# A graph network on one core: destination rows are added onto source rows by an accumulating DMA instead of by VectorE

## The chip, the core and the metric

The kernel runs on 1 core of a Trainium2 chip (trn2). The metric is device time in microseconds of one execution, the median of several runs. The profile is one execution, taken by the hardware profiler; its times count from the span's start.

## What is computed

The reference takes 3125 nodes with 256 features, 53125 edges (sorted by destination) with 128 features each, and runs four graph blocks, each followed by a residual sum and a layer norm. The change lies in the first, the edge network:

```
h = concat(x[src], x[dst])                     # per edge, 512 wide
h = tanh(h @ W0 + b0)                          # 512 -> 406
h = tanh(h @ W1 + b1)                          # 406 -> 323
h = h @ W2 + b2                                # 323 -> 256
h = h * (edge_attr @ Wg)                       # 128 -> 256, a gate
out = mean of h over the edges of each source node
x = layernorm(x + out)
```

The other three blocks are a GCN pair, three SAGE layers, and a mean aggregation of a linear layer, all on the same edges.

## The kernel before, in words

**Tables.** Because `concat(x[src], x[dst]) @ W0` is a sum of two products, a setup stage (25 tiles of 128 nodes, loop over `n < T`) computes two tables in HBM, `p_tab = x @ W0[:256]` and `q_tab = x @ W0[256:] + b0`, with rows of `H1 = 416` float32 numbers. For each tile TensorE (PE) runs 12 matmuls (L272 to L274), ScalarE (ACT) copies one half out of PSUM (L329) and VectorE (DVE) adds `b0` to the other (L398). The setup also counts the edges per bucket. It ends near 107 us.

**Edge stage.** 53248 edges (padded) are worked in `G = 104` groups of `GC = 4` chunks of `C = 128` edges. The stage is a software pipeline: each engine has one `body(t)` for turn t, written out by hand in the engine's own order and run by `edge_loop` (a few turns unrolled, then a hardware loop of 2 turns per iteration, then a few turns). `t.group(k)` is the group that is k ahead of the turn's own. In turn t:

- GpSimd (POOL) issues 12 indirect DMAs of 128 rows each: four gathers of source rows (`p_tab` to `p_in`) and four of destination rows (`q_tab` to `q_in`) for group t+3 (`gather`, L617), and four scatters of finished messages for group t-2 (`scatter`, L624). Between the three bursts of four it waits: for `s_L2` and `s_add` ahead of the first, for `s_L1` (TensorE has finished the first third of the layer W1 of group t) ahead of the second, for `s_place`, `s_L2` and `s_msg` ahead of the third.
- VectorE adds the two rows of group t+2, chunk by chunk (`add`, two instructions: L834 for 384 columns, L837 for the last 32 columns, which it writes four times side by side, so that `pre1` has 512 columns). It also takes the low halves of the hidden layers for the split products (`first_low` L853 and L855, `second_low` L867), the one-hots and places (L878 to L898), and the message, product times gate (L906).
- TensorE transposes `pre1` of group t+1 (L673, four per chunk), runs W1 on group t (`first`, L679 to L681 and L695) and W2 and the gate product on group t-1 (`second`, L679 to L681 and L712), and the rank products (L716).
- ScalarE runs tanh of the first hidden layer (L772, L774), of the second (L786, L789) and copies the gate out of PSUM (L798).

All of `pre1` and the gate lie in `R_buf`; `p_in`, `q_in` and `pre1` have two slots each. Two PSUM banks serve the second product: TensorE's `second(t, 2)` waits until the message of chunk 0 has been read out (`s_msg`), which waits for ScalarE's gate copy, which waits for TensorE's `s_L2`.

**After it** (from 2170 us): one-hot matmuls that build the counts and sum the messages, and the three further blocks. The change doesn't touch them, beyond where `pre1` is stored.

## Time and profile before

| what | value |
| --- | --- |
| median of 3 runs | 3755.33 us (3738.34, 3755.33, 3803.82) |
| span of the profiled execution | 3707.1 us |
| lowest run less that span | 31.2 us |
| median less that span | 48.2 us |
| busy: PE, DVE, ACT, POOL | 3298.7, 2156.1, 1576.1, 1363.5 us |
| edge stage (first gather to last scatter) | 108.5 to 2162 us |

How to read it: the profile gives no device time of its own beside its span, so what lies around the span is known only as the difference to the runs. Busy times are sums over the whole span; the edge stage is a little over half of it, and almost all of POOL's work lies there. The three runs differ by 1.7%.

### The profile page before, as it was taken

Reading aid. Unit: us, or ns where it says so; the run is one execution under the profiler, and the core shown is the slowest. Engines: PE = TensorE matmul, PEld = TensorE weight load, DVE = VectorE, ACT = ScalarE, POOL = GpSimd, SP = SyncE. Lnnn points to the kernel's source line nnn. Section 1 sums busy time; section 2 is a strip of 40 time slices with the busy share of each in tenths; the row PEclk is TensorE's granted clock in tenths of the full one; section 3 lists DMA queues with packets and bytes.
Section 4 is the critical chain, followed back from the end, with each engine's and each line's share of the span. In section 5 each row is a group of like instructions: output and inputs, shape, how many; then the busy total and the mean of one; then the engine's idle time right before and its main releaser. Section 6 shows DMA issues by size and latency. Waiting matters only on the chain. (4 is left out here: it accounts for less than half of the span.)

```text
span 3707.1 us, 68629 instructions
## 1 busy us (share of the span) xinstructions
PE 3298.7 (89%) x19277; PEld 2783.2 (75%) x19278; DVE 2156.1 (58%) x5404; ACT 1576.1 (43%) x3210; POOL 1363.5 (37%) x1410
## 2 busy tenths in 40 slices
PE   7688888888888888888888889899999999999999
PEld 6466766777767666767676766777888999999888
DVE  7566666666666665666666668899444211124422
ACT  2344545554555444555454547777111111111244
POOL 2556666666666555666665422222000000000000
PEclk9799999999999999999999989999999999999999
DMA  4444444444444433444444368888755666666465
GB/s 159 138 124 129 129 129 130 136 132 126 134 133 134 124 119 118 129 132 132 135 125 120 97 190 254 253 263 264 228 176 176 205 210 211 205 218 203 144 206 163
DMA packets 288343, 605.46 MB, mean 163 GB/s; under 512 B 38577, under 2 KB 195850, under 8 KB 288266
## 3 DMA queue, kind: packets, MB, share of 16 engines
q1 hardware_dynamic: 170848, 321.14, 28.0%
q0 software_dynamic: 73216, 232.67, 20.7%
q10 hardware_dynamic: 44202, 50.63, 4.0%
q8 instruction: 47, 0.77, 0.1%
q14 instruction: 30, 0.25, 0.0%
HBM read 493.97 MB, written 110.32 MB: 163 GB/s over the span
## 5 line engine op out<-in xcount | busy, mean ns | idle before, releaser
L998 PE MATMUL bank<-ring,parts 128*128 128x320 f32 x4000 | 641.6, 316 | 5.4 <-issue 2.5
L998 PEld LDWEIGHTS bank<-ring,parts 128*128 128x128 f32 x4000 | 595.1, 188 | 16.3 <-issue 10.9
L679 PE MATMUL bank<-w2h,hidden2h 108*128 108x256 f32 x1248 | 421.0, 337 | 143.1 <-DVE rows_out L906 112.0
L624 POOL DMA_INDIRECT msgs<-rows_out,sidx x416 | 427.5, 1028 | 306.9 <-PE bank L712 157.4
L617 POOL DMA_INDIRECT p_in<-p_tab,gidx x416 | 402.1, 967 | 289.2 <-issue 125.6
L617 POOL DMA_INDIRECT q_in<-q_tab,gidx x416 | 408.7, 982 | 231.3 <-issue 116.1
L679 PE MATMUL bank<-hidden1h,w1h 128*108 128x512 f32 x936 | 422.1, 451 | 23.7 <-DVE hidden2l L867 22.0
L679 PEld LDWEIGHTS bank<-w2h,hidden2h 108*128 108x128 f32 x1248 | 248.6, 199 | 194.0 <-DVE rows_out L906 142.4
L680 PE MATMUL bank<-hidden1l,w1h 128*108 128x512 f32 x936 | 382.6, 409 | 0.1
L681 PE MATMUL bank<-hidden1h,w1l 128*108 128x512 f32 x936 | 380.0, 406 | 0.0
L681 PE MATMUL bank<-w2h,hidden2l 108*128 108x256 f32 x1248 | 366.1, 293 | 4.2 <-issue 4.1
L673 PE MATMUL bank<-ident,R_buf 128*128 128x128 f32 x1664 | 254.3, 288 | 128.5 <-DVE hidden1h L855 97.2
L786 ACT ACTIVATE hidden2h<-bank,b1c 108x512 fp32r<-108x512 f32 (+1 forms) x312 | 215.2, 690 | 359.2 <-remote 177.3
L680 PE MATMUL bank<-w2l,hidden2h 108*128 108x256 f32 x1248 | 365.4, 293 | 2.9 <-issue 2.9
L1135 PE MATMUL bank<-at_dst,at_src 128*128 128x320 f32 x1088 | 324.8, 380 | 36.9 <-DVE at_src L1107 29.8
L867 DVE TENSOR_TENSOR hidden2l<-bank,hidden2h 108x512 fp32r<-108x512 f32 (+1 forms) x312 | 215.6, 691 | 234.8 <-ACT bank L789 216.6
L673 PEld LDWEIGHTS bank<-ident,R_buf 128*128 128x128 f32 x1664 | 209.3, 149 | 177.5 <-issue 134.5
L772 ACT ACTIVATE hidden1h<-bank 128x512 fp32r<-128x512 f32 x416 | 247.4, 595 | 216.3 <-remote 139.4
L798 ACT COPY R_buf<-bank 128x256 f32<-128x256 f32 x416 | 148.2, 376 | 439.6 <-PE bank L712 292.7
L1139 PE MATMUL bank<-R_buf,at_src 128*128 128x257 f32 x1088 | 325.1, 380 | 0.0
L906 DVE TENSOR_TENSOR rows_out<-bank,R_buf 128x256 f32<-128x256 f32 x416 | 166.6, 421 | 258.6 <-ACT R_buf L798 179.4
L1101 DVE TENSOR_SCALAR at_dst<-T_buf,R_buf 128x640 fp32r<-128x640 f32 x544 | 303.9, 559 | 11.5 <-PE bank L1139 9.3
(243 smaller groups left out, 6137.6 us busy)
## 6 DMA issues: line engine op xcount, KB each, us to landing
ring<-counts SPq DMA_DIRECT2D x250, 800.0 KB, 4.3
R_buf<-msgs SPq DMA_DIRECT2D x544, 130.0 KB, 3.0
counts<-cells ACTq DMA_DIRECT2D x125, 320.0 KB, 3.4
eT<-in_edge_T SPq DMA_DIRECT2D x104, 256.0 KB
p_in<-p_tab,gidx POOLq DMA_INDIRECT x416
q_in<-q_tab,gidx POOLq DMA_INDIRECT x416
msgs<-rows_out,sidx POOLq DMA_INDIRECT x416
p_tab<-p_out SPq DMA_DIRECT2D x25, 208.0 KB, 1.9
```

Of the source, the lines that this page charges most:

```text
L617: pool.indirect_dma_start(out=rows_in[:, z, c], out_offset=None, in_=tab[:], in_offset=bass.IndirectOffsetOnAxis(ap=gidx[:, z, which, c:c ...
L624: pool.indirect_dma_start(out=msgs[:], in_=rows_out[:, z, c], in_offset=None, out_offset=bass.IndirectOffsetOnAxis(ap=sidx[:, z, c:c + 1], ...
L673: mm = pe.transpose(bT[c % 2][:, k * C:(k + 1) * C], pre1[:, z, c, k * P:(k + 1) * P], ident[:])
L679: pe.matmul(out, lh.bitcast(F32R), rh.bitcast(F32R), start=first, stop=False)
L680: pe.matmul(out, lh.bitcast(F32R), rl.bitcast(F32R), start=False, stop=False)
L681: return pe.matmul(out, ll.bitcast(F32R), rh.bitcast(F32R), start=False, stop=last)
L772: act.activation(hidden1h[:, z, :, e].bitcast(F32R), src, ACT.Tanh).then_inc(s_hi1, 1)
L867: v.tensor_tensor(hidden2l[0:rows_m, z, m].bitcast(F32R), bH[m % 2][0:rows_m, :], hidden2h[0:rows_m, z, m], ALU.subtract).then_inc(s_lo2, 1)
L998: mm = pe.matmul(banks[q][:, 0:NW], part[:, TB * i + a, h * P:(h + 1) * P].bitcast(dt), ring[:, slot, a].bitcast(dt), start=first and x == ...
L1101: v.tensor_scalar(at_dst[:, u % HOTS].bitcast(F32R), iota[:], rows[:, u % RS, D + 2:D + 3], None, ALU.is_equal)
L1135: pe.matmul(bank[:, half * 512:half * 512 + 2 * CW][:, bass.ds(at[u], NW)], at_src[:, u % HOTS].bitcast(F32R), at_dst[:, u % HOTS, half * ...
L1139: pe.matmul(bS[:, bass.ds(at[u], SW)], at_src[:, u % HOTS], rows[:, u % RS, 0:SW], start=False, stop=False, skip_group_check=True).then_in ...
```

## The change

VectorE's `add` goes. POOL first gathers the source rows straight into `pre1`, and one turn later gathers the destination rows onto them with an accumulating indirect DMA (`compute_op=ALU.add`), so that `pre1` is complete when the DMA has landed. `pre1` gets its own buffer with a ring of four slots (`RING`), with source rows fetched four groups ahead and destination rows three. `p_in` and `q_in` go. Since nothing writes the last 32 columns four times any more, the tables themselves have 512 columns (`H1W`): W0 and b0 are widened on the host by repeating those columns, and the setup's matmuls, copies and table writes are 512 wide. POOL waits for `s_p_rows` (source rows landed) and `s_T` (slot transposed) where it waited for `s_add`; TensorE waits for `s_q_rows`, one semaphore for two chunks, where it waited for `s_add`. The copy of the row numbers (`table_rows`) moves to after `first_low(t, 3)`. POOL, TensorE and VectorE run hardware loops of four turns instead of two. The message scatters share one semaphore per slot.

```diff
--- before.py
+++ after.py
@@
+H1W = H1T * P
...
+RING = 4
...
-        p_tab, q_tab = dram("p_tab", [NP, H1]), dram("q_tab", [NP, H1])
+        p_tab, q_tab = dram("p_tab", [NP, H1W]), dram("q_tab", [NP, H1W])
...
-                                to, q = psum[2 * (n % 3) + half][:, 0:H1], 2 * half + k
+                                to, q = psum[2 * (n % 3) + half][:, 0:H1W], 2 * half + k
...
-                        act.copy(p_out[:, j], psum[2 * (n % 3)][:, 0:H1]).then_inc(s_pe, 1)
+                        act.copy(p_out[:, j], psum[2 * (n % 3)][:, 0:H1W]).then_inc(s_pe, 1)
...
-                        v.tensor_tensor(q_out[:, n % TB], psum[2 * (n % 3) + 1][:, 0:H1], b0_b[:],
+                        v.tensor_tensor(q_out[:, n % TB], psum[2 * (n % 3) + 1][:, 0:H1W], b0_b[:],
...
-            p_in, q_in = (esb(n, [P, 2, GC, H1]) for n in ("p_in", "q_in"))
-            pre1 = R_buf[:, 0:2 * GC * H1T * P].rearrange("p (z c n) -> p z c n", z=2, c=GC)
-            gate = R_buf[:, 2 * GC * H1T * P:][:, 0:GC * D].rearrange("p (c n) -> p c n", c=GC)
-            gidx = esb("gidx", [P, 2, 2, GC], I32)
+            pre1 = esb("pre1", [P, RING, GC, H1W])
+            gate = R_buf[:, 0:GC * D].rearrange("p (c n) -> p c n", c=GC)
+            gidx = esb("gidx", [P, RING, 2, GC], I32)
...
-            s_in_rows = [[esem(f"s_in_rows{z}{c}") for c in range(GC)] for z in range(2)]
-            s_sc = [[esem(f"s_sc{z}{c}") for c in range(GC)] for z in range(2)]
+            s_p_rows = [esem(f"s_p_rows{z}") for z in range(2)]
+            s_q_rows = [[esem(f"s_q_rows{y}{h}") for h in range(GC // 2)] for y in range(RING)]
+            s_sc = [esem(f"s_sc{z}") for z in range(2)]
             s_eT = [esem(f"s_eT{z}") for z in range(2)]
-            s_idx, s_add, s_T, s_th1, s_lo1 = (esem(n) for n in ("s_idx", "s_add", "s_T", "s_th1", "s_lo1"))
+            s_idx, s_T, s_th1, s_lo1 = (esem(n) for n in ("s_idx", "s_T", "s_th1", "s_lo1"))
...
-                def gather(t, c, tab, which, rows_in):
-
-                    z = t.slot(3)
-                    pool.indirect_dma_start(out=rows_in[:, z, c], out_offset=None, in_=tab[:],
-                                            in_offset=bass.IndirectOffsetOnAxis(ap=gidx[:, z, which, c:c + 1], axis=0)
-                                            ).then_inc(s_in_rows[z][c], 16)
+                def gather_source(t, c):
+
+                    y = t.ring(4)
+                    pool.indirect_dma_start(out=pre1[:, y, c], out_offset=None, in_=p_tab[:],
+                                            in_offset=bass.IndirectOffsetOnAxis(ap=gidx[:, y, 0, c:c + 1], axis=0)
+                                            ).then_inc(s_p_rows[t.slot(4)], 16)
+
+                def add_destination(t, c):
+
+                    y = t.ring(3)
+                    pool.indirect_dma_start(out=pre1[:, y, c], out_offset=None, in_=q_tab[:],
+                                            in_offset=bass.IndirectOffsetOnAxis(ap=gidx[:, y, 1, c:c + 1], axis=0),
+                                            compute_op=ALU.add).then_inc(s_q_rows[y][c // 2], 16)
 
...
                 def body(t):
 
                     if t.has(-2) and t.has(1):
                         pool.wait_ge(s_L2, t.group(-2) * GC + 3)
-                    if t.has(3):
-                        pool.wait_ge(s_idx, t.group(3) + 1)
-                        wait(pool, s_add, (t.group(3) - 1) * GC)
+                    if t.has(4):
+                        pool.wait_ge(s_idx, t.group(4) + 1)
+                        wait(pool, s_T, (t.group(4) - RING + 1) * GC)
                         stand_alone(pool, s_up)
                         for c in range(GC):
-                            gather(t, c, p_tab, 0, p_in)
+                            gather_source(t, c)
                     if t.has(0):
                         pool.wait_ge(s_L1, H2T * t.group(0) + 1)
+                        if not t.has(3):
+                            stand_alone(pool, s_up)
+                    if t.has(3):
+                        pool.wait_ge(s_p_rows[t.slot(3)], 16 * GC * (t.use(3) + 1))
                         stand_alone(pool, s_up)
-                    if t.has(3):
                         for c in range(GC):
-                            gather(t, c, q_tab, 1, q_in)
+                            add_destination(t, c)
...
-                edge_loop(pool, body, -3, 4, G - 4, G + 2)
+                edge_loop(pool, body, -4, 4, G - 4, G + 2, RING)
...
-                    pe.wait_ge(s_add, j * GC + c + 1)
+                    pe.wait_ge(s_q_rows[t.ring(1)][c // 2], 32 * (t.ring_use(1) + 1))
...
-                        mm = pe.transpose(bT[c % 2][:, k * C:(k + 1) * C], pre1[:, z, c, k * P:(k + 1) * P], ident[:])
+                        mm = pe.transpose(bT[c % 2][:, k * C:(k + 1) * C], pre1[:, t.ring(1), c, k * P:(k + 1) * P],
+                                          ident[:])
...
-                edge_loop(pe, body, -1, 3, G - 1, G + 1)
+                edge_loop(pe, body, -1, 3, G - 1, G + 1, RING)
...
-                def table_rows(z, g):
+                def table_rows(y, g):
 
                     at = bass.ds(g * GC, GC)
-                    v.tensor_copy(gidx[:, z], edge_i[:, :, at]).then_inc(s_idx, 1)
-
-                def add(t, c):
-
-                    j, z = t.group(2), t.slot(2)
-                    if not t.has(2):
-                        return
-                    v.wait_ge(s_in_rows[z][c], 32 * (t.use(2) + 1))
-                    wait(v, s_T, (j - 2) * GC + c + 1)
-                    if c == GC - 1 and t.has(4):
-                        table_rows(z, t.group(4))
-                    full, rest = slice(0, H1F * P), slice(H1F * P, H1)
-                    v.tensor_tensor(pre1[:, z, c, full], p_in[:, z, c, full], q_in[:, z, c, full], ALU.add)
-
-                    copies = [P, P // H1R, H1R]
-                    v.tensor_tensor(pre1[:, z, c, H1F * P:].rearrange("p (r n) -> p r n", n=H1R),
-                                    p_in[:, z, c, rest].unsqueeze(1).broadcast_to(copies),
-                                    q_in[:, z, c, rest].unsqueeze(1).broadcast_to(copies), ALU.add
-                                    ).then_inc(s_add, 1)
+                    v.tensor_copy(gidx[:, y], edge_i[:, :, at]).then_inc(s_idx, 1)
 
...
-                    add(t, 0)
                     second_low(t, 0)
                     places(t)
                     first_low(t, 2)
-                    add(t, 1)
                     second_low(t, 1)
                     first_low(t, 3)
-                    add(t, 2)
+                    if t.has(1) and t.has(5):
+                        table_rows(t.ring(5), t.group(5))
                     message(t, 0)
                     message(t, 1)
-                    add(t, 3)
                     second_low(t, 2)
...
-                edge_loop(v, body, -2, 3, G - 5, G + 1)
+                edge_loop(v, body, -1, 3, G - 5, G + 1, RING)
...
+    def repeated(a):
+        return np.concatenate([a] + [a[:, H1F * P:]] * (P // H1R - 1), axis=1)
+
+    W0 = repeated(padded(w["L0_gnn_W0"], (2 * D, H1)))
```

## Rows read from the trace of the kernel before

**Rows 1.** The page's part 2: 40 slices of the span, in tenths.

```profile
POOL 2556666666666555666665422222000000000000
PEclk9799999999999999999999989999999999999999
```

**Rows 2.** Busy time in three stretches: the edge stage, then its last gathers, then behind them.

```profile
core 0: us, PE busy (x) PEld busy (x) DVE busy (x) ACT busy (x) POOL busy (x), PEclk, DMA share, GB/s
187.00:2100.00 1913.00, 1639.51 (x9414) 1323.12 (x9413) 1260.69 (x3045) 960.54 (x1770) 1169.65 (x1178) 0.94 0.43 128
2080.00:2100.00 20.00, 16.08 (x95) 13.28 (x94) 12.24 (x30) 9.82 (x18) 11.44 (x12) 0.91 0.42 125
2100.00:2110.00 10.00, 10.00 (x64) 8.16 (x63) 7.17 (x18) 6.66 (x12) 2.38 (x3) 1.00 0.20 67
```

**Rows 3.** Timeline of the last gather, and of two successive turn ends on PE (L716, rest_b).

```profile
2093.81 0.95 POOL L617 DMA_INDIRECT q_in<-q_tab,gidx  x1 [0.30 <-issue]
...
2104.05 0.37 PE L716 MATMUL bank<-in_bucket,rest_b 128*128 128x500 bf16 x1
...
2119.28 0.37 PE L716 MATMUL bank<-in_bucket,rest_b 128*128 128x500 bf16 x1
```

**Rows 4.** PE's waits from 187 to 2100 us: in total, times, longest.

```profile
PE bank L679 <- DVE rows_out L906: 108.1, 60, 3.1
PE bank L673 <- DVE hidden1h L855: 90.2, 28, 5.3
```

**Rows 5.** Timeline of one late chain, PE to ACT to DVE to PE.

```profile
1031.51 0.60 PE L712 MATMUL bank<-wg,eT 128*128 128x256 f32 x2
...
1036.02 0.97 POOL L624 DMA_INDIRECT msgs<-rows_out,sidx  x1 [0.30 <-issue]
...
1036.77 0.37 ACT L798 COPY R_buf<-bank 128x256 f32<-128x256 f32 x1 [5.36 <-PE bank L712]
1037.17 0.42 DVE L906 TENSOR_TENSOR rows_out<-bank,R_buf 128x256 f32<-128x256 f32 x1 [2.93 <-issue]
...
1037.65 0.39 PE L679 MATMUL bank<-w2h,hidden2h 108*128 108x256 f32 x1 [1.59 <-DVE rows_out L906]
```

**Rows 6.** Timeline of another, with an addition ahead of the message on DVE.

```profile
767.67 0.56 DVE L834 TENSOR_TENSOR R_buf<-p_in,q_in 128x384 f32<-128x384 f32 x1
...
768.46 0.76 DVE L906 TENSOR_TENSOR rows_out<-bank,R_buf 128x256 f32<-128x256 f32 x2
...
768.94 0.39 PE L679 MATMUL bank<-w2h,hidden2h 108*128 108x256 f32 x1 [2.17 <-DVE rows_out L906]
```

**Rows 7.** Groups by line: the additions, the gathers and the scatters (busy, mean ns of one, idle before).

```profile
L624 POOL DMA_INDIRECT msgs<-rows_out,sidx x416 | 427.5, 1028 | 306.9 <-PE bank L712 157.4 <-issue 113.9 <-DVE rows_out L906 24.0
L617 POOL DMA_INDIRECT q_in<-q_tab,gidx x416 | 408.7, 982 | 231.3 <-issue 116.1 <-remote 67.2 <-PE bank L695 44.9
L617 POOL DMA_INDIRECT p_in<-p_tab,gidx x416 | 402.1, 967 | 289.2 <-issue 125.6 <-PE bank L712 72.0 <-DVE R_buf L837 52.6
...
L834 DVE TENSOR_TENSOR R_buf<-p_in,q_in 128x384 f32<-128x384 f32 x416 | 232.0, 558 | 19.5 <-DMA q_in<-q_tab,gidx 10.1
...
L837 DVE TENSOR_TENSOR R_buf<-p_in,q_in 128x128 f32<-128x128 f32 x416 | 119.0, 286 | 0.0
```

**Rows 8.** Timeline: an issue on POOL beside an addition on DVE, and one without.

```profile
1006.00 0.56 DVE L834 TENSOR_TENSOR R_buf<-p_in,q_in 128x384 f32<-128x384 f32 x1
...
1006.23 1.15 POOL L617 DMA_INDIRECT p_in<-p_tab,gidx  x1 [0.30 <-issue]
...
1008.94 0.95 POOL L617 DMA_INDIRECT q_in<-q_tab,gidx  x1 [0.30 <-issue]
```

**Rows 9.** DMA queue of POOL's transfers, 1000 to 1400 us: packets, MB, share of 16 engines.

```profile
q0 software_dynamic: 14385, 45.73, 37.6%
```

**Rows 10.** Timeline: two successive setup matmuls, POOL's first destination gather, the first transposes.

```profile
65.10 0.35 PE L272 MATMUL bank<-w0h,xh 128*128 128x416 f32 x1
...
65.28 0.36 PE L273 MATMUL bank<-w0l,xh 128*128 128x416 f32 x1
...
113.82 0.95 POOL L617 DMA_INDIRECT q_in<-q_tab,gidx  x1 [0.31 <-issue]
...
118.09 2.25 PE L673 MATMUL bank<-ident,R_buf 128*128 128x128 f32 x8 [12.54 <-DVE R_buf L837]
```

**Rows 11.** The page's part 3: the queue of TensorE's instruction pages, whole span.

```profile
q8 instruction: 47, 0.77, 0.1%
```

More of the change, by code:

```diff
@@ L171, in build @@
                 s_spread = ssem("s_spread")
-                w0, w0h, w0l = (ssb(n, [P, 2 * KD, H1]) for n in ("w0", "w0h", "w0l"))
+                w0, w0h, w0l = (ssb(n, [P, 2 * KD, H1W]) for n in ("w0", "w0h", "w0l"))
                 xh, xl = (ssb(n, [P, 3, KD, P]) for n in ("xh", "xl"))
                 s_w0h, s_w0l, s_xh, s_xl = (ssem(n) for n in ("s_w0h", "s_w0l", "s_xh", "s_xl"))
-                b0_b = ssb("b0_b", [P, H1])
+                b0_b = ssb("b0_b", [P, H1W])
                 xt = ssb("xt", [P, TB, KD, P])
-                p_out = ssb("p_out", [P, TB, H1])
-                q_out = ssb("q_out", [P, TB, H1])
+                p_out = ssb("p_out", [P, TB, H1W])
+                q_out = ssb("q_out", [P, TB, H1W])
                 xf, qf, rf, mf = (ssb(n, [P, 2, G * GC]) for n in ("xf", "qf", "rf", "mf"))
@@ L583, in use, with ring, ring_use, edge_loop @@
                 def use(self, k):
-                    return self.it + (self.a + k) // 2
+                    return self.step // 2 * self.it + (self.a + k) // 2
+                def ring(self, k):
+                    return (self.a + k) % RING
+                def ring_use(self, k):
+                    assert self.step == RING
+                    return self.it + (self.a + k) // RING
                 def has(self, k):
                     return not isinstance(self.it, int) or 0 <= self.group(k) < G
-            def edge_loop(eng, body, first, head, tail, last):
+            def edge_loop(eng, body, first, head, tail, last, step=2):
                 for i in range(first, head):
-                    body(Turn(0, i))
-                assert (tail - head) % 2 == 0
-                with eng.Fori(0, (tail - head) // 2) as it:
-                    for u in range(2):
-                        body(Turn(it, head + u))
+                    body(Turn(0, i, step))
+                assert (tail - head) % step == 0
+                with eng.Fori(0, (tail - head) // step) as it:
+                    for u in range(step):
+                        body(Turn(it, head + u, step))
                 for i in range(tail, last):
-                    body(Turn(0, i))
+                    body(Turn(0, i, step))
             @blk.sync
@@ L656, in body @@
                             scatter(t, c)
-                edge_loop(pool, body, -3, 4, G - 4, G + 2)
+                edge_loop(pool, body, -4, 4, G - 4, G + 2, RING)
                 for z in range(2):
-                    for c in range(GC):
-                        pool.wait_ge(s_sc[z][c], 16 * (G // 2))
+                    pool.wait_ge(s_sc[z], 16 * GC * (G // 2))
             @blk.tensor
@@ L894, in places @@
                     ch.link(v.tensor_reduce(place[:], ranked[:], mybir.AxisListType.X, ALU.add))
-                    for c in range(GC):
-                        wait(v, s_sc[z][c], 16 * t.use(-1))
+                    wait(v, s_sc[z], 16 * GC * t.use(-1))
                     v.tensor_copy(sidx[:, z], place[:])
@@ L926, in body @@
                     message(t, 3)
-                for z in range(2):
-                    table_rows(z, z)
+                for y in range(RING):
+                    table_rows(y, y)
                 v.memset(hidden2h[:], 1.0).then_inc(s_one, 1)
```

15 lines of the change are left out of this document (7 added, 8 removed).

## The prediction, made before the changed kernel had run

> **What bounds the kernel now.** I read the page's slices first. They show where POOL works: the second to the 22nd slice, which is the edge stage [rows 1]. The change touches only this stage and the setup ahead of it, so everything behind 2170 us is left out. The windows come next. From 187 to 2100 us PE is busy 1639.5 of 1913.0 us at a granted clock of 0.94 of 2.4 GHz [rows 2]. POOL ran 1178 indirect DMAs there, 12 per turn, so 98.2 turns of 19.5 us each.
>
> The telling rows are at the stage's end. POOL issues its last gather at 2093.81 [rows 3]. In the 20 us around it PE is busy for 16.08 us at 0.91; in the 10 us behind it PE is busy for 10.00 of 10.00 us at 1.00 [rows 2]. The two ends of turn there lie 2119.28 - 2104.05 = 15.2 us apart [rows 3]. VectorE still makes additions in that turn. So PE's own work is 15.2 us per turn, and 19.5 - 15.2 = 4.3 us per turn (420 us in all) are lost while POOL is issuing gathers, additions or not.
>
> Who loses them is in the waits: PE idles 273.5 us (1913.0 less 1639.5), 2.8 us per turn, above all for messages (L906, 108.1 us in 60 waits) and for the low halves of the first hidden layer (L855, 90.2 us in 28) [rows 4]. The other 1.5 us per turn are work at the lower clock, which comes with the idling. So a microsecond of idling costs 4.3 / 2.8 = 1.5 us. One chain shows how a wait arises: PE's L712 matmuls begin at 1031.51 and take 0.60 us, yet ScalarE, idle for 5.36 us and put down to PE, starts only at 1036.77; then VectorE's message at 1037.17, then PE at 1037.65 [rows 5]. VectorE was idle for 2.93 us in it: no addition stood in the way. PE's signal reached ScalarE some 4.7 us after the matmul; POOL was issuing its scatter of 1036.02 just before. I conclude that the stage is bound by PE plus late signals, that these are tied to POOL's issue, and that VectorE is a link of the chain, seldom its slow one.
>
> **The change, part by part.** The sum is made on the profiled span, 3707.1 us, and carried over to the median, 48.2 us higher; the terms are differences.
>
> (1) The additions go. That frees 558 + 286 = 844 ns per chunk, 3.4 us of VectorE per turn [rows 7], nearly all beside PE's work. What counts is an addition between a late signal and the message that PE waits for. In one chain the additions start at 767.67, the messages at 768.46 and PE's wait ends at 768.94 [rows 6]: 0.8 of its 2.17 us go, and next late is ScalarE's gate copy. In the other chain nothing goes [rows 5]. The 60 waits at L906 so give between 0 and 60 x 0.84 = 50 us. I take 40, nearer the upper end, because PE's 28 listed waits at L855 and the unlisted short ones sometimes have an addition ahead too. With the clock's part: 40 x 1.5 = 60 us. **-60 us** (0 to -75).
>
> (2) POOL's issue beside additions. An issue beside an addition took 1.15 us, one without 0.95 [rows 8], but the means of all gathers are only 967 and 982 ns [rows 7], 0.02 to 0.03 above the 0.95. That is 0.2 us of POOL per turn. How much a microsecond of POOL is worth I take as a proportion: 4.3 us lost for 12 x (0.98 + 0.30) = 15.3 us of issuing, 0.28. So 0.2 x 0.28 x 98 = **-5 us**.
> The Trainium skill ("SBUF — State Buffer", "Who interferes with whom") says that a VectorE instruction with two SBUF inputs contends with a GpSimd instruction that reads SBUF, the one issued later being blocked; by that each of four additions would hold POOL up for up to 0.84 us, 3.4 us per turn, and their going would give 3.4 x 0.28 x 98 = 93 us. The measured 0.2 us in 1.15 against 0.95, and the means, speak for the small value.
>
> (3) The accumulating DMAs. Before there are 12 issues per turn, and there are 12 after. The trace has no accumulating DMA. The lower bound is a plain gather, 0.98 + 0.30 us; the upper is two of them, +1.28 us. The nearest row but the gather itself is the scatter, 1.028 us [rows 7], 0.05 more. An accumulating row has a second address to read, though, so I take +0.25 us, half of what half as many addresses again would make of 0.98. Four per turn: 1.0 x 0.28 x 98 = **+27 us** (0 to +140; above that POOL itself binds, see the rivals).
>
> (4) Their transfers. POOL's queue takes 37.6% of 19.5 us, 7.3 us per turn [rows 9]. By bytes, 8 x 1664 of 8 x 1664 + 4 x 1040 are the gathers', so one gather takes 0.70 us of all 16 engines, and at 2048 bytes a row 0.86 us, below the 1.28 us from one issue to the next: hidden, and if the cover went it would cost 0.16 x 8 x 0.28 x 98 = 35 us. The accumulating ones take between 0.86 and twice that, for the second read: 1.72 us against 1.53 from issue to issue, which leaves 0.8 us at the end of a run of four. **+10 us** (0 to +22).
>
> (5) New waits. POOL's wait for source rows is for rows issued a turn earlier; queued behind it are four accumulating DMAs and four scatters. At 19.5 us per turn against a few us of landing it costs nothing. POOL's wait for L837 (52.6 us before p gathers, [rows 7]) goes, but its next wait in that place, for PE's L712, is nearly as late (72.0 us). PE's wait for destination rows has nearly two turns of cover. The row-number copy moves on VectorE alone. Loops of four turns: no more than the 47 instruction pages of TensorE at 0.1% of 16 engines over 3707 us, 1.3 us each, pass in the whole run [rows 11], so loops of two turns are not fetched anew; I take the same for four.
>
> (6) Setup. Two matmuls of 416 columns start 0.18 us apart at full clock [rows 10]; 96 more columns add 0.043 us, for 12 x 25 matmuls **+13 us** (VectorE's and ScalarE's longer evictions, a tenth of a us each, raise the upper end to 18).
>
> (7) Start. The first transposes waited for additions fed by the fifth to eighth DMA [rows 10]. Now four more gathers come first, 5.0 us, and the wait is for a pair of chunks, 1.3 us more, less an addition of 0.8: **+6 us**.
>
> Sum: -60 - 5 + 27 + 10 + 13 + 6 = -9 us; 3755 - 9 = 3746. No term is known to better than 5 us, so I forecast 3745, own range 3680 to 3800.
>
> **The rivals.**
> *POOL becomes the bound (slower).* If an accumulating issue costs the full +1.28 us, a turn has 12 x 1.28 + 4 x 1.28 = 20.5 us of issuing, and of POOL's idle time now (19.5 - 15.3 = 4.2 us) at least some stays, since each run waits for PE: I take 1.5. Turn 22.0, +2.5 x 98 = 245 us, plus 19 of (6) and (7): 4000 us. At +0.7 us a DMA POOL's 18.1 us plus 1.5 reach the present turn; from there it decides. For: POOL is already 78% issued. Against: the scatter costs hardly more than the gather.
>
> *VectorE was the slow link (faster).* If freeing a quarter of VectorE's time lets it absorb the late signals, so that all waits for messages go, that is 108.1 x 1.5 = 162 us; with terms (3) to (7) in part, 3755 - 162 + 19 = 3612, up to 3650. For: the message waits are the largest. Against: full speed with additions behind the last gather, and VectorE's 2.93 us idle in [rows 5].
>
> *The added reading floods the DMA queue.* An accumulating row reads two sources, so its transfer takes 1.72 us, issues stay at 1.28 and each run of four drains 1.8 us late: 1.8 x 0.28 x 98 = 48 us in place of term (3) and (4), 3770; if the late signals follow the transfers one for one, 1.8 x 98 = 175 us, 3870.
> The Trainium skill ("Collectives: The Full Stack", "The bandwidth ceiling: the fold count and why AG ≠ RS ≠ AR") states that a reducing DMA runs at half the rate of a copy because it needs two source reads, measured 1.93 to 1; no row here shows an accumulating DMA yet.
>
> *The change doesn't hide what it moves.* PE waits for landed rows, or loops of four turns overrun the instruction store: 25 iterations x 3 pages x 1.3 us = 98 us, 3840.
>
> **How the numbers follow.** The forecast has 0.42, POOL-bound 0.20, VectorE the slow link 0.20, flooded queue 0.12, not hidden 0.06. A measurement of this kernel tells some 2% (75 us) from no change; the three runs alone spread by 1.7%. Faster by over 2% (below 3680): 0.20 and 0.03 of the forecast's tail, 0.23. Slower (above 3830): 0.20, a third of the flooded queue (0.04), 0.05 of the last rival and 0.01 of the forecast's tail, 0.30. Within: 0.47. The range leaves out 0.08 of the fast rival and 0.11 of the slow one: 3625 to 3970. The likeliest case's own range is 3680 to 3800.
>
> **What the profile will show.** L834 and L837 are gone and VectorE's busy time in the edge stage is 3.4 us per turn lower. The mean of the accumulating issue says which case holds: below 1.3 us mine, above 1.7 us POOL-bound. The waits at L906 shrink by a third and those at L855 don't. ScalarE still idles 3 to 5 us behind some of the L712 while POOL issues. The turn is 19 to 19.6 us. The queue's share rises from 37.6% to 45 to 60%. The prediction is wrong if late signals have another cause than POOL's issue, or if an accumulating DMA is dear.

## The result, and the profile of the changed kernel

The changed kernel took 3817.44 us (median of 4 runs, 3792.65 to 3831.77), the kernel before 3753.93 us (4 runs). By the medians it is 63.5 us or 1.7% slower; the ratio on record is 1.022 (95%: 1.0159 to 1.028). Ratios in this document use only those runs that lie within 1.5% of their kernel's fastest, so they can differ from the quotient of the medians beside them. The forecast was 3745, -9 us. The time lies in the outer range given (3625 to 3970) and outside the likeliest case's own (3680 to 3800), and the sign is wrong. The profiled execution took 3824.44 us (span 3822.7).

The windows view of the edge stage answers [rows 2]:

```profile
core 0: us, PE busy (x) PEld busy (x) DVE busy (x) ACT busy (x) POOL busy (x), PEclk, DMA share, GB/s
187.00:2100.00 1913.00, 1571.06 (x8864) 1279.75 (x8863) 940.53 (x2118) 906.34 (x1658) 1299.62 (x1116) 0.91 0.60 140
```

POOL ran 1116 indirect DMAs, 93.0 turns of 20.57 us, against 19.5 before. PE now idles 342 us of the 1913 (273.5 before), at a lower clock. VectorE was indeed relieved: 10.1 us of work per turn where it had 12.8, 2.7 us less (3.4 were forecast). Groups by line, for [rows 7]:

```profile
L633 POOL DMA_INDIRECT pre<-q_tab,gidx x416 | 645.7, 1552 | 310.9 <-remote 206.7 <-issue 100.1 <-PE bank L714 3.0
L640 POOL DMA_INDIRECT msgs<-rows_out,sidx x416 | 408.8, 983 | 247.8 <-PE bank L731 134.6 <-issue 106.1 <-DVE rows_out L906 5.8
L626 POOL DMA_INDIRECT pre<-p_tab,gidx x416 | 399.6, 960 | 158.5 <-issue 144.5 <-DVE gidx L841 13.4 <-PE bank L691 0.3
```

An accumulating issue (L633) takes 1552 ns, the plain gather (L626) 960. With the 0.30 us in front of each, the 12 issues of a turn make 17.6 us, so POOL still pauses 2.9 of the 20.57 us. PE's waits from 187 to 2100 us, for [rows 4]:

```profile
PE bank L691 <- DVE hidden1h L856: 313.0, 83, 4.9
...
PE bank L698 <- DVE rows_out L906: 5.2, 5, 2.1
```

The message waits are all but gone (5.2 us after 108.1), as term (1) said and more. In their place stands one wait in nearly every turn, 83 in 93, of 3.8 us, in front of a transpose (L691). The timeline of one such turn shows how it arises (start, us, idle before):

```profile
1013.88 1.03 PE L691 MATMUL bank<-ident,pre 128*128 128x128 f32 x8
...
1014.68 0.99 POOL L626 DMA_INDIRECT pre<-p_tab,gidx  x1 [0.30 <-issue]
...
1018.49 0.94 POOL L626 DMA_INDIRECT pre<-p_tab,gidx  x1 [0.30 <-issue]
1019.43 0.60 ACT L791 ACTIVATE hidden1h<-bank 128x512 fp32r<-128x512 f32 x1 [5.29 <-remote]
...
1021.34 0.29 DVE L856 TENSOR_TENSOR hidden1h<-bank,hidden1h 32x128 fp32r<-32x128 f32 x1
...
1021.68 0.69 PE L691 MATMUL bank<-ident,pre 128*128 128x128 f32 x2 [4.24 <-DVE hidden1h L856]
1021.79 1.59 POOL L633 DMA_INDIRECT pre<-q_tab,gidx  x1 [2.35 <-remote]
```

PE ends the first two blocks of transposes at 1014.9. ScalarE has been idle for 5.29 us and starts on them only at 1019.43, at the end of POOL's last issue, 4.5 us after the matmuls. It is the late signal of [rows 5], at another place (a signal is the semaphore increment by which an instruction tells other engines that it is done). VectorE isn't what holds ScalarE up: it waits too. At the start of the stage, for [rows 10]:

```profile
133.18 1.12 PE L691 MATMUL bank<-ident,pre 128*128 128x128 f32 x4 [19.81 <-DMA pre<-q_tab,gidx]
```

That is 15.1 us later than before; 8.0 of them are the setup (POOL's first gather at 116.54 after 108.51), 7.1 the longer way to the first rows.

### The profile page after: what moved, and what is told of

It reads as the page before. It is cut to its first block and busy times, and to the rows that moved or that the text cites. A ratio compares the mean times of both kernels' runs of the same rounds, so it can differ in the third digit from the quotient of the medians.

```text
span 3822.7 us, 66546 instructions
## 1 busy us (share of the span) xinstructions
PE 3334.3 (87%) x19277; PEld 2817.6 (74%) x19278; DVE 1883.5 (49%) x4572; ACT 1584.5 (41%) x3210; POOL 1580.5 (41%) x1410
## 5 line engine op out<-in xcount | busy, mean ns | idle before, releaser
L633 POOL DMA_INDIRECT pre<-q_tab,gidx x416 | 645.7, 1552 | 310.9 <-remote 206.7
L691 PE MATMUL bank<-ident,pre 128*128 128x128 f32 x1664 | 272.5, 302 | 373.4 <-DVE hidden1h L856 331.1
L691 PEld LDWEIGHTS bank<-ident,pre 128*128 128x128 f32 x1664 | 218.8, 156 | 431.6 <-DVE hidden1h L856 357.4
L626 POOL DMA_INDIRECT pre<-p_tab,gidx x416 | 399.6, 960 | 158.5 <-issue 144.5
L698 PE MATMUL bank<-hidden1h,w1h 128*108 128x512 f32 x936 | 456.9, 488 | 1.4 <-issue 1.4
L699 PE MATMUL bank<-hidden1l,w1h 128*108 128x512 f32 x936 | 414.9, 443 | 0.0
L698 PE MATMUL bank<-w2h,hidden2h 108*128 108x256 f32 x1248 | 400.2, 321 | 12.5 <-DVE rows_out L906 7.8
L700 PE MATMUL bank<-hidden1h,w1l 128*108 128x512 f32 x936 | 410.2, 438 | 0.0
L854 DVE TENSOR_TENSOR hidden1l<-bank,hidden1h 128x384 fp32r<-128x384 f32 x416 | 231.8, 557 | 290.9 <-ACT bank L793 236.3
L1133 PEld LDWEIGHTS bank<-at_dst,at_src 128*128 128x128 f32 x1088 | 188.1, 190 | 122.5 <-issue 85.2
```

Of the source, the lines that this page charges most:

```text
L626: pool.indirect_dma_start(out=pre1[:, y, c], out_offset=None, in_=p_tab[:], in_offset=bass.IndirectOffsetOnAxis(ap=gidx[:, y, 0, c:c + 1], ...
L633: pool.indirect_dma_start(out=pre1[:, y, c], out_offset=None, in_=q_tab[:], in_offset=bass.IndirectOffsetOnAxis(ap=gidx[:, y, 1, c:c + 1], ...
L691: mm = pe.transpose(bT[c % 2][:, k * C:(k + 1) * C], pre1[:, t.ring(1), c, k * P:(k + 1) * P], ident[:])
L698: pe.matmul(out, lh.bitcast(F32R), rh.bitcast(F32R), start=first, stop=False)
L699: pe.matmul(out, lh.bitcast(F32R), rl.bitcast(F32R), start=False, stop=False)
L700: return pe.matmul(out, ll.bitcast(F32R), rh.bitcast(F32R), start=False, stop=last)
```

## Experiments

**Two conditions.** The kernel before itself didn't run alike in all rows of runs. Where three or four kernels ran one after the other on the chip beside it, it took 3271 us in each of three rows; where one kernel ran beside it, 3739 to 3867 us in each of seven (and 3754 where the prediction's runs were made). One chip gave both. In the eleven traces of the quick condition PE's signals are on time: at least 1323 of the 1334 increments in the edge stage are recorded within 0.06 us of their matmul's end. In the nine others it is 432 to 904 of some 1337 (688 in the changed kernel). The granted clock is 1.00 in the edge stage on time, but 0.97 in h0 and f5, where PE waits for another reason (below). I call the conditions "on time" and "late". Each kernel is compared with the kernel before of its own row. The prediction was made for "late".

The late traces differ in one more thing. All nine lack 13 to 29% of the records of semaphore increments by instructions in the edge stage, and 41 to 62% of those by landing DMAs (the kernel before has 4324 for 5625 increments); the eleven others lack at most 0.3% of the first kind. So who ended a wait is less certain in them than how long it was. And one rival to every cause named here is not excluded: that the recording itself, and not only the kernel, makes the signals late. Every run on record carries a span and a granted clock, so none shows the kernel without it. What sets the condition stays open.

All kernels of the study add register operations in the stage behind the edge stage: bounds asserted on the counts that ScalarE and VectorE load (names with e) or a mask to 12 bits (the others). g5, g6 and h0 have the mask and, on ScalarE's load, the asserted bound too, which f5 and a0 don't: by the traces the stage behind takes 1557 to 1565 us in these three, against 1545 to 1552 in the others with the mask. Against its nearest kin each loses 12 to 15 us there (h0 to f5, g6 to b0, g5 to a0), which are of that edit and not of the change.

| kernel | on time: us (before 3271) | late: us / before of its row, ratio (95%) |
|---|---|---|
| before, masked (b0) | 3272.2, 1.0003 | |
| changed (h0; a0) | 3540.3, 1.082 (1.0805-1.0841) | 3786 / 3741, 1.014 (1.009-1.019) |
| changed, plain destination gathers (f1; g1) | 3282.4, 1.0029 | 3887 / 3843, 1.012 (1.003-1.022) |
| changed, no source gathers (f4; g4) | 3275.9, 1.0014 | 3329 / 3743, 0.890 (0.883-0.897) |
| changed, run of issues broken (f5; g5) | 3525.5, 1.077 | 3669 / 3867, 0.962 (0.949-0.975); medians 0.949 |
| changed, VectorE burdened again (g7) | | 3848 / 3770, 1.020 by the medians, no interval |
| before, no additions (f2; g2) | 3263.2, 0.9974 | 3834 / 3739, 1.022 (1.014-1.031) |
| before, wide rows (h3) | 3281.6, 1.0030 | |
| before, run of issues broken (g6) | | 3808 / 3858, 1.005 (0.998-1.012); medians 0.987 |

**First row: e0 to e4.** Only the edit in the stage behind, and then one part each.

> The kernel before, with bounds asserted on the counts that ScalarE and VectorE load in the stage behind the edge stage, as all the kernels that follow have it. It measures what that edit costs by itself. Both theories: nothing, 3754 us within 10 us (at most 3775, if the assertions cost 1 us a word of the table).

> The changed kernel with plain destination gathers: the destination rows overwrite the source rows, and the addition is left out. Theory A, the issue price of the accumulating gather (1552 ns against about 970 ns plain): four of them a turn give back 2.3 us of POOL's unbroken run, the turn falls from 20.6 to about 18.3 to 19.3 us, and the time to 3600 to 3700 us. Theory B, the accumulation costs elsewhere (the transposes wait for rows that land late): the issue falls to 0.97 us, and the turn falls only if the transposes were waiting for rows, which the trace of after doesn't show; 3800 us or more. Theory C, the stall at the transposes is ScalarE's and VectorE's own chain and has nothing to do with POOL: 3817 us, unchanged.

```diff
-  in_offset=..., compute_op=ALU.add).then_inc(s_q_rows[y][c // 2], 16)
+  in_offset=...).then_inc(s_q_rows[y][c // 2], 16)
```

> The kernel before with each addition cut to 16 columns (the rest of the addition is left out; gathers, waits and row width as before). It measures VectorE's relief alone. Theory A, the prediction's first term: the message waits of 4.3 us a turn shrink by a third or more, 3754 - 60 = 3694 us. Theory B, relief only moves the stall to the transposes behind POOL's run, as in the changed kernel: the wait at the message matmuls is gone, one of 2 to 4 us stands at the transposes, and the time is 3735 to 3754 us.

```diff
-  v.tensor_tensor(pre1[:, z, c, full], p_in[:, z, c, full], q_in[:, z, c, full], ALU.add)
-  ... (the 128 repeated columns)
+  v.tensor_tensor(pre1[:, z, c, 0:16], p_in[:, z, c, 0:16], q_in[:, z, c, 0:16], ALU.add)
```

> The changed kernel without its source gathers: 8 instead of 12 indirect DMAs a turn; the source rows are left out of the sum. Theory A, PE's signals of the transposes reach ScalarE only when POOL's unbroken run of DMA issues ends: POOL has 12 us of issue in the turn, pauses while PE works at the transposes, the signals come on time and the stall of about 4 us in front of a transpose goes; the turn falls from 20.6 to 16 to 17 us and the time to 3420 us (3370 to 3500). Theory C, the stall is the chain PE, ScalarE, VectorE by itself: the stall stays, at most 0.05 us a turn is won, 3790 to 3817 us.

```diff
-  for c in range(GC):
-      gather_source(t, c)
...
-  pool.wait_ge(s_p_rows[t.slot(3)], 16 * GC * (t.use(3) + 1))
```

Measured 3330.4, 3335.1, 3319.6 and 3327.7 us beside 3271.2. The asserted bounds cost 59 us, all expectations missed that, and against e0 nothing moved by more than 11 us: the row was on time, and PE was busy all through the stage. Since the stall under question wasn't there, the row couldn't tell the theories apart. From here on the mask took the place of the bounds.

**The changed kernel, late (a0).**

> The changed kernel, with the loaded counts of the stage behind the edge stage masked to 12 bits (one more register operation for each; nothing else). The kernel before took 3271 us on the chip of the first four runs and 3754 us where the prediction's runs were made. If the difference is a regime in which PE's signals come late, then: where the kernel before takes some 3270 us, TensorE has no idle time in the edge stage, the change saves nothing and costs its setup and start, +10 to +25 us (3280 to 3296 us), and the accumulating gather's 1.55 us hides, since POOL has 12 of 15.4 us (14.2 with the dearer issue). Where the kernel before takes some 3750 us: 3817 us again, ratio 1.016 to 1.028. Rival: the accumulating issue binds in the fast regime too (14.2 us of issue and its waits in a turn of 15.4 us): +100 us or more there.

3786 us, ratio 1.014: the result repeated, with PE's wait at L691 in 84 of 94 turns.

**No additions in the kernel before (f2, g2): the first term alone.**

> The kernel before with each addition cut to 16 columns (the rest left out), with the masked counts: VectorE's relief alone. Where PE's signals come late: the prediction's first term says 3740 - 60 = 3680 us; the rival, that the relief only moves PE's stall to the transposes, says 3725 to 3745 us. Where they come on time: TensorE bounds the turn, 3265 to 3275 us.

> The same kernel as f2_no_additions (the kernel before with each addition cut to 16 columns, the rest left out), run by itself with the kernel before, in the condition in which PE's signals come late. Theory of the prediction's first term: the waits for VectorE's messages shrink, 3740 - 60 = 3680 us. Theory F, the waits were never VectorE's own work but late signals of PE in front of it, and a shorter VectorE only meets them earlier: 3720 to 3745 us, with PE's idle time moved to the transposes.

Late, taking VectorE's additions away made the kernel 2.2% slower (3834 us beside 3739, some +84 by the ratio), beyond both expectations; on time 8 us faster. PE's waits of g2 from 187 to 2100 us, and one turn of it:

```profile
PE bank L673 <- DVE hidden1h L849: 327.3, 83, 4.9
PE bank L679 <- DVE rows_out L900: 10.0, 6, 3.3
```
```profile
1014.72 0.99 POOL L617 DMA_INDIRECT p_in<-p_tab,gidx  x1 [0.59 <-issue]
1015.38 1.03 PE L673 MATMUL bank<-ident,R_buf 128*128 128x128 f32 x8
...
1018.54 0.95 POOL L617 DMA_INDIRECT p_in<-p_tab,gidx  x1 [0.30 <-issue]
1020.68 0.60 ACT L772 ACTIVATE hidden1h<-bank 128x512 fp32r<-128x512 f32 x1 [3.93 <-remote]
```

It is the changed kernel's pattern, with no accumulating DMA and no wide row in it. PE gets its messages in time, so it comes early enough to end its transposes (1016.4) each turn within POOL's run of scatters and source gathers, and their signal comes 4.3 us later, 1.2 us behind the end of the run. In the kernel before that happened in 28 turns of 98 [rows 4].

**Plain destination gathers (f1, g1): the price of accumulating.** Destination rows overwrite source rows; the addition is left out.

> The changed kernel with plain destination gathers (destination rows overwrite source rows; the addition is left out) and the masked counts of a0_after. Where PE's signals come late (kernel before at some 3740 us, a0_after 3786 us): theory A, the late signals are released when POOL's unbroken run of issues ends, so 2.3 us less issue a turn bring them forward: 98 x 1 to 2.3 us less, 3560 to 3690 us. Theory D, plain issues every 1.27 us hold the signals more than accumulating ones every 1.85 us (the signals during the accumulating gathers were on time): then nothing is won, 3740 to 3830 us. Where they come on time (before at 3271 us): 3285 us in both, as e1_plain_destination less its dearer bounds.

> The same kernel as f1_plain_destination (plain destination gathers, the addition left out), run by itself with the kernel before, in the condition in which PE's signals come late (the kernel before at some 3740 us; the changed kernel with masked counts took 3786 us, turn 20.6 us; without source gathers 3329 us). Theory A, what the signals wait for is the end of POOL's unbroken run, which is 2.3 us shorter: turn 18.3 to 19.3 us, 3560 to 3680 us, so that the accumulating issue is what makes the change a loss. Theory D, plain issues at 1.27 us spacing hold the signals more than accumulating ones at 1.85 us: turn 20 to 21 us, 3740 to 3830 us, and the price of the accumulating issue is worth nothing.

Late, it gave nothing: 1.012 beside 1.014, the same pattern (346.7 us in 85 waits at the transposes). The 3887 us lie above both expectations, as the kernel before took 3843 in that row. Theory A falls in its simple form. Theory D, that plain issues hold the signals more, would fit, but no run tested it alone. On time, it gave everything, as the changed kernel itself shows there:

> The changed kernel with the masked counts again, this time with two more kernels in the same row of runs. In both rows of four kernels the kernel before took 3271 us and PE's signals came on time; in every row of one kernel it took 3740 us or more and they came late. If the row decides, the kernel before takes 3271 us here, TensorE has no idle time in the edge stage, and the changed kernel takes 3280 to 3296 us (plain gathers in place of the accumulating ones took 3282). If it does not: some 3786 us against 3740.

Here my expectation was wrong, and the rival named before a0 right (the accumulating issue binds on time too): 3540 us, not 3280 to 3296. Windows and group of h0, and of f1:

```profile
187.00:1650.00 1463.00, 1328.79 (x7954) 1091.47 (x7953) 816.03 (x1900) 822.00 (x1491) 1159.75 (x995) 0.97 0.72 164
...
L633 POOL DMA_INDIRECT pre<-q_tab,gidx x416 | 646.2, 1553 | 126.8 <-issue 123.4
```
```profile
187.00:1650.00 1463.00, 1462.94 (x9228) 1227.65 (x9227) 954.67 (x2212) 954.02 (x1731) 1111.37 (x1155) 1.00 0.63 190
...
L633 POOL DMA_INDIRECT pre<-q_tab,gidx x416 | 393.6, 946 | 128.9 <-issue 116.1
```

995 DMAs in 1463 us are turns of 17.64 us in h0; 1155 are turns of 15.20 us in f1. POOL's issues with the 0.30 us between them make 4 x 1.85 + 4 x 1.26 + 4 x 1.28 = 17.6 us in h0: POOL issues without a pause and is the bound, and PE waits for it by way of the messages (134.2 us in 81 waits at L698). In f1 the 12 issues make 15.2 us, and PE is busy 1462.94 of 1463. The same windows of the kernel before (b0) and of the changed kernel without source gathers (f4):

```profile
187.00:1650.00 1463.00, 1462.88 (x9186) 1218.40 (x9186) 1219.15 (x2967) 947.59 (x1721) 1112.32 (x1147) 1.00 0.56 163
```
```profile
187.00:1650.00 1463.00, 1463.00 (x9227) 1228.39 (x9226) 955.83 (x2211) 953.51 (x1732) 977.14 (x770) 1.00 0.61 121
```

f4 has 8 DMAs a turn and POOL pauses in it; its turn is 15.20 us, so that is PE's own work. b0's is 15.31 us, and POOL fills it: 1112.3 us of issues and 1147 pauses of 0.30 to 0.31 us are the whole 1463. So on time the kernel before was already issuing without a pause, 0.1 us a turn above PE's work, and any dearer issue had to lengthen its turn. The timeline of h0, POOL in an unbroken run:

```profile
1001.36 0.39 PE L698 MATMUL bank<-w2h,hidden2h 108*128 108x256 f32 x1 [2.14 <-DVE rows_out L906]
...
1001.82 1.59 POOL L633 DMA_INDIRECT pre<-q_tab,gidx  x1 [0.30 <-issue]
...
1003.72 1.55 POOL L633 DMA_INDIRECT pre<-q_tab,gidx  x1 [0.30 <-issue]
...
1009.25 1.02 POOL L640 DMA_INDIRECT msgs<-rows_out,sidx  x1 [0.30 <-issue]
...
1010.58 1.00 POOL L640 DMA_INDIRECT msgs<-rows_out,sidx  x1 [0.30 <-issue]
```

The transfers didn't bind. POOL's queue, 1000 to 1400 us, in h0 and in f1:

```profile
q0 software_dynamic: 24698, 59.61, 64.8%
```
```profile
q0 software_dynamic: 21938, 69.39, 56.3%
```

That is 11.4 and 8.6 us per turn, 0.72 us more for each accumulating DMA. By bytes a plain one takes 0.85 in f1, so an accumulating one takes 1.57, 1.84 times as much, and fits into its 1.85 us of issue. (This is an estimate: it puts all of the difference between the two queues down to the accumulating ones.) The Trainium skill ("Collectives: The Full Stack", "The bandwidth ceiling: the fold count and why AG ≠ RS ≠ AR") has 1.93 for a reducing DMA against a copy; the trace nearly agrees, and yet on time it is not the transfer but the issue that costs.

**No source gathers (f4, g4): fewer issues.** Source rows are left out of the sum.

> The changed kernel without its source gathers (source rows are left out of the sum; 8 indirect DMAs a turn instead of 12), with the masked counts. Where PE's signals come late: theory A, POOL's run is 12.3 us instead of 17.3 and starts when PE reaches its transposes' neighbourhood with a pause of 3 us or more, the late signals go, the turn falls from 20.6 to 16 to 17 us, 3380 to 3480 us. Theory E, the signals are late for another reason that POOL's issues don't set (a slower memory, other cores): as many late as before, 3740 us or more. Where they come on time: 3285 us in both.

> The same kernel as f4_no_source, run by itself with the kernel before. Twice the kernel before took 3271 us and PE's signals came on time (with four kernels in a row on the chip), twice it took 3740 to 3755 us and they came late (by itself with one kernel). If the condition is of that kind, the kernel before takes some 3740 us here. Then theory A, POOL's run of 12 us leaves a pause and the signals come on time: 3380 to 3480 us. Theory E, the signals come late whatever POOL issues: 3700 us or more. If the kernel before takes 3271 us, it repeats f4_no_source at 3276 us, and the condition is none of the order of the runs.

Late, 3329 us: 457 us less than a0, better than theory A said. Windows, waits and one turn of g4:

```profile
187.00:1700.00 1513.00, 1479.64 (x9220) 1226.30 (x9219) 963.50 (x2209) 944.50 (x1729) 975.71 (x769) 1.00 0.59 117
```
```profile
PE bank L690 <- DVE hidden1h L855: 32.6, 59, 0.9
```
```profile
1015.93 0.96 POOL L640 DMA_INDIRECT msgs<-rows_out,sidx  x1 [0.30 <-issue]
1016.73 1.03 PE L690 MATMUL bank<-ident,pre 128*128 128x128 f32 x8
1017.81 0.60 ACT L790 ACTIVATE hidden1h<-bank 128x512 fp32r<-128x512 f32 x1 [0.75 <-PE bank L690]
...
1020.92 1.60 POOL L633 DMA_INDIRECT pre<-q_tab,gidx  x1 [4.03 <-PE bank L713]
```

With 8 DMAs a turn (769 / 8 = 96.1 turns of 15.7 us) POOL has finished when PE ends its transposes and pauses for 4.03 us. The signal is at most 0.7 us late there, the idle time nearly gone, the clock back at 1.00. The condition is still "late": the kernel before beside it takes 3743 us, and of g4's own PE increments only 904 of 1337 are on time. So with four issues fewer the delays shrink: they hang on what POOL issues. The load on the DMA engines is hardly the reason, as their share is 0.59 in g4 and 0.60 in the changed kernel. Four issues fewer are 5.0 us of POOL and gave 4.7 us a turn.

**A run broken (f5, g5 in the changed kernel, g6 in the one before).**

> The changed kernel with one wait moved: POOL issues its four source gathers only when PE's second block of transposes of the same turn has signalled (s_T two counts later), so that POOL's run of 12 issues is cut into 8 and 4; and the masked counts. Where PE's signals come late: theory A, the signals of the two transposes come within 1 us as POOL stands, PE's 3.75 us stall in front of the transposes goes, the turn falls from 20.6 to 17.5 to 19 us: 3490 to 3640 us. Theory D (a queue that plain issues fill and that empties slowly): the signals still come 3 to 5 us late, and the wait costs POOL that time: 3800 to 4000 us. Where they come on time: nothing, 3285 us.

> The same kernel as f5_break_after (the changed kernel, source gathers behind PE's second transposes), by itself with the kernel before. Where PE's signals came on time it took 3525 us, a turn of 17.9 us set by POOL's chain (source gathers, their landing, accumulating gathers, scatters). Theory A: broken runs keep the signals on time, so it takes the same 3500 to 3600 us where they come late in the kernel before (some 3740 us). Theory D: with 12 issues a turn the signals come late in any grouping, and the time is 3750 us or more.

```diff
-  wait(pool, s_T, (t.group(4) - RING + 1) * GC)
+  wait(pool, s_T, (t.group(4) - RING + 1) * GC + 2 if t.has(1) else 0)
```

> The kernel before with one wait more: POOL issues its four source gathers only when PE's second block of transposes of the turn has signalled, so that scatters and source gathers are no longer one run of 8; masked counts; by itself with the kernel before. Theory A (PE's signals are held while POOL's run goes on beyond its first four or five issues, and let go some 2 us after it ends): the signals of the first two transposes come on time, the stalls of 4.3 us a turn shrink by half or more, turn 16.5 to 18.5 us, 3450 to 3650 us. Theory D (how many issues a turn there are decides, not their grouping): the wait costs POOL its pause, 3740 to 3950 us.

```diff
   wait(pool, s_add, (t.group(3) - 1) * GC)
+  if t.has(1):
+      wait(pool, s_T, t.group(1) * GC + 2)
```

g5 won 3.8% (5.1% by the medians), less than theory A said, at turns of 19.1 us (1201 DMAs in 1913 us), with the number of issues unchanged. On time (f5) the moved wait was met whenever POOL came to it and broke nothing. POOL issues in one unbroken run as in h0, the group of source gathers having only the 0.30 us in front of each:

```profile
L626 POOL DMA_INDIRECT pre<-p_tab,gidx x332 | 318.8, 960 | 101.2 <-issue 100.9 <-PE bank L731 0.3
```

Its edge stage is as long as h0's (1858 us both); of the 15 us between them (3525 and 3540) 12 are the asserted bound. My expectation of 3285 us failed there as in h0. g6 decided nothing by its time. PE's waits of g6, 187 to 2100 us:

```profile
PE bank L681 <- DVE rows_out L908: 234.0, 84, 6.4
PE bank L681 <- issue: 51.5, 17, 5.1
```

The stall at the transposes is gone and one of 2.8 us stands at the messages in 84 turns: the broken run had been scatters and source gathers, and now source and destination gathers follow each other unbroken. That these hold the signals of PE's second layer is how I read it, and not shown. (By the ratio g6 is 0.5% slower, by the medians 1.3% quicker: the kernel before scattered from 3773 to 3891 us in that row.)

**VectorE burdened again in the changed kernel (g7).**

> The changed kernel with VectorE's four additions a turn put back in their places, on a scratch buffer (same shapes, no waits, their sums used by nothing), and the masked counts; by itself with the kernel before. g2_no_additions showed that taking the additions out costs the kernel before 2.2% where PE's signals come late. Theory F: the relief of VectorE is what makes the change slower, through the time at which PE reaches its transposes against POOL's run. Then putting the work back wins: ratio to before 0.995 to 1.005 instead of 1.014, turn 19.3 to 19.8 us, some 3740 us. Theory G: relief and accumulating gathers act each for itself and VectorE's work costs time again: the turn grows from 20.4 to 21 us or more, ratio 1.02 to 1.05.

```diff
+  own = R_buf[:, GC * D:GC * D + 6 * H1W].rearrange("p (k n) -> p k n", k=6)
+  v.tensor_tensor(own[:, 2 + c, full], own[:, 0, full], own[:, 1, full], ALU.add)
+  ... (and the 128 repeated columns), four times a turn
```

PE's waits of g7:

```profile
PE bank L691 <- DVE hidden1h L868: 291.7, 80, 5.1
PE bank L698 <- DVE rows_out L918: 40.1, 20, 3.1
```

Theory F falls: the work put back didn't bring back the old pattern, and 1.020 is no gain over 1.014 (the kernel before scattered from 3698 to 3794 us in that row, so more than the lack of a gain can't be read from it). Theory G, that VectorE's work costs time of its own again, isn't excluded: the turn is 20.7 us (1107 DMAs) where a0 has 20.4. VectorE's relief is enough to bring the stall about in the kernel before, but its burden doesn't remove it from the changed one.

**Wide rows alone, and the mask alone (h3, b0).**

> The kernel before with tables, weights and gathered rows of 512 instead of 416 columns (additions and everything else as before), and the masked counts: the prediction's setup, start and transfer terms alone. Prediction: +13 for the setup, and of the transfers' +10 what the width brings: +13 to +25 us where PE's signals come late, 3753 to 3765 us. Where they come on time: the setup alone, +8 to +15 us, 3280 to 3290 us. Rival: the wide rows hold PE's signals longer, +40 us or more where they come late.

> The kernel before with nothing but the masked counts, to show what that edit costs in the kernels of this study that carry it: 0 to 10 us, all of it in the stage behind the edge stage, in either condition.

On time: +10.5 us for the width, within what was expected, and +1.0 us for the mask. The wide rows alone were not run late.

## Why the prediction was wrong

**What bounds the kernel** was read rightly for the runs predicted, as far as the runs show: PE plus late signals tied to POOL's issue (g4). That the same kernel has a condition without them, 13% quicker, could not be seen from one trace.

**Term (1), "-60 us", is the step that failed**, in sign. The rows were right as far as they went: the message waits went from 108.1 to 5.2 us, by more than the 40 taken. The unsaid assumption was that a wait which goes leaves all others where they are. With late signals it doesn't: PE comes to its transposes earlier, within POOL's run, and pays there (313.0 us for 90.2). The relief alone measured 1.022 (g2), as large as the whole change: some +84 us where -60 was forecast. It isn't the whole account of the changed kernel, whose stall stays when VectorE is burdened again (g7). I had asked in (5) what is next late for POOL, but not in (1) for PE, and had named PE's L855 waits as untouched by the change.

**Term (3), "+0.25 us each, +27 us"**: the issue costs +0.58 us, more than twice my value, inside the bound of 1.28. Its conversion, 0.28 us lost per us of POOL, failed in both directions: 2.3 us a turn were worth nothing measurable late (g1) and 2.4 us a turn on time (f1 to h0, 258 us, 11 of them the asserted bound); 5.0 us of whole issues were worth 4.7 late (g4). A ratio of two totals of one trace is no price.

**The rival "POOL becomes the bound"** wasn't reached late: the issue costs +0.58 us, below the +0.7 that it asked for, and POOL still pauses 2.9 us a turn (up to 2.35 at one place above). On time it is exactly what happens, at +0.58 us already, as POOL had no pause left there (b0).

**The range** held by luck: it reaches up to 3817 us only for rivals (bound by POOL, flooded queue) that were not what happened late. Their prices were also added up wrongly in part: the flooded queue comes to 3757 and 3884 us by its own terms where 3770 and 3870 are given, and the bound by POOL to 4019 where 4000 is.

**The rest.** (2): beside additions and without them the gathers took 964 and 959 against 960 and 946 ns on time (e0, f2), with the scatters some 0.1 us a turn, so the small value was right; the 93 us that I had drawn from the Trainium skill's rule ("SBUF — State Buffer", "Who interferes with whom") were not there. The same section adds that this kind of addition was seen not to stall DMAs, so the rule didn't ask for them either. (4): the queue's share rose to 54.6% of a turn, as forecast, and its transfer, estimated at 1.57 us an accumulating DMA on time, fits into the 1.85 us of its issue. (5): no wait for rows, no fetched loops (49 instruction pages for 47). (6) and (7): +8.0 and +7.1 us at the start for +13 and +6; h3 has +10.5 for the width. The turn was forecast at 19 to 19.6 us and is 20.57.

**Still open:** why PE's signals come late in one condition and not in the other, and whether they would without the recording; and what, besides VectorE's relief, keeps the changed kernel in its pattern, as g7 and g1 both stay in it. That POOL spends its issue in runs matters (g5, g6), but no rule for the delay by the length of a run was shown.

## What to carry to other kernels

Where an engine's signals come late while another engine issues, a wait that you remove can be found again at the next handover inside that engine's run (g2): ask which signal falls into the run once the engines ahead are quicker, and try the relief alone before you pay for it. Count the issue time of the engine that issues the DMAs per turn before giving it a dearer kind: 15.3 us of issuing beside PE's 15.2 left room for nothing on time. Moving work from VectorE into a DMA pays only if the issuing engine has the time; here four issues fewer gave 12% late, and all of VectorE's additions gone gave 0.3% on time.

## What the runs showed of the hardware

- An accumulating indirect DMA of 128 rows of 2048 bytes takes POOL 1.55 to 1.56 us to issue, a plain one 0.95 to 0.98, whether rows have 1664 or 2048 bytes.
- PE's signals came up to 5 us late (4.3 and 4.5 in the turns shown) in the stage in which POOL issues indirect DMAs, in every trace of the late condition, and never in the setup or behind the edge stage (48 of 48 and 1286 of 1286 increments within 0.06 us in the changed kernel); with 8 DMAs a turn in place of 12 the delay shown is 0.7 us.
- The traces with late signals lack 13 to 29% of the records of semaphore increments of that stage, the others at most 0.3%.
- The same kernel took 3271 us in some rows of runs and 3739 to 3867 us in others, 14 to 18% more.
